# A state-space layer and a gated recurrence on one Trainium2 core: kernel setup and first states re-placed among the row statistics

## The chip, the cores and the metric

The kernel runs on one core of a Trainium2 chip as a single launch. The metric is the device time of the launch in microseconds. TensorE, VectorE, ScalarE, GpSimd and SyncE are called PE, DVE, ACT, POOL and SP, as in the profile. Each engine takes its own list of instructions strictly in order. An instruction that waits for a semaphore holds back everything behind it on its engine.

## The reference

Two sandwiched layers over x of shape (8, 2048, 512) in float32, cut to what matters:

```python
# first layer: layer norm, a diagonal-plus-low-rank state-space convolution, gelu
K  = _dplr_kernel(Bc, Cc, Pc, Qc, Lam, step_c, seq_len)        # (512, 2048)
Kf = jnp.fft.rfft(K, n=2 * seq_len, axis=-1)
uf = jnp.fft.rfft(r, n=2 * seq_len, axis=1)                    # r = _layernorm(x)
h1 = jnp.fft.irfft(uf * Kf.T[None], n=2 * seq_len, axis=1)[:, :seq_len]
x  = x + _layernorm(gelu(h1 + D[0] * r))
# second layer: layer norm, a gated recurrence over the first axis, a product, tanh
c  = sigmoid(xt @ wf.T + c @ uf.T + bf) * c + sigmoid(xt @ wi.T + c @ ui.T + bi) * tanh(xt @ wc.T + c @ uc.T + bc)
h  = tanh(x @ wo.T + c_final @ uo.T + bo)
x  = x + _layernorm(h)
```

## The kernel before

The convolution is done in 16 chunks of 128 steps. Inside a chunk it is a product with a triangular matrix T of samples of K. Across chunks it goes through a state of 128 numbers for each channel: `Gm` carries a chunk's input into the state, the power of the state matrix in `Ak` carries the state on, and the output matrix M reads it out. Channels are taken in 16 groups of 32. For group 0 there are 15 states (`state(0)` to `state(14)`) and 12 pieces of M (`outm(0, 0)` to `outm(0, 11)`), each made by PE, then rounded to a high f16 half by ACT (lines 1061 and 1072), then completed by a low half by DVE (lines 1428 and 1438). Every state but the first needs both halves of the state before it. `state(1)` and all after it also wait for `ak` 8, which is the eighth power of the state matrix split into halves by POOL (`power(7)`, lines 908 and 835).

**The stage in question** is the first 136 us, the row statistics. It reads x chunk by chunk (16 chunks, k from 0 to 15, three buffers `xt`) to get the mean and variance of each row. Of the eight rows per partition in a chunk DVE takes `NB` (`rows_of`: 4, 5 or 6; 5 for chunks 5 to 11, 6 from chunk 12) with one `bn_stats` each (line 1448) and one `bn_aggr` each (line 1460), and ACT takes the rest with a `total` pass (line 1039), a `mean` (lines 1043, 1044) and a `square_sum` pass (line 1049), closed by `var` (line 1097). POOL turns the variances of a chunk into inverse deviations (lines 934, 936) and then normalizes the inputs u of the first groups: `norm(n)` in quarters of a group (two instructions, lines 918 and 920) and, for the last four chunks of group 0, `norm_chunk(k)` (lines 927, 929). `norm(2)` makes the inputs of states 8 to 11. It stands in POOL's program behind the variance of chunk 11. SP loads chunk k when chunk k - 3 is done by both DVE and ACT (`load_x`, line 536).

**Between the chunks** DVE does the serial work that makes the matrices. `square(0)` to `square(6)` double a power of the state matrix (line 1348) and store it (line 1334); each needs a product by PE. `kernel_out`, `kernel_max` and `kernel_parts` (lines 1392 to 1422) take the samples of K, find powers of two for scaling, and write `Cst` and its halves `C16` (lines 1416 to 1418, the start of M), `Gm` (line 1420) and the scaled samples (line 1422, semaphore `kparts`), which SP stores to `kpad`, from where T is loaded.

**EARLY** says behind which chunk's statistics the first 14 states are made. In DVE a state follows rows 0, 2, 4 and the last of the chunk. In ACT the first state of a chunk stands ahead of the chunk's `total` pass (`early()` at line 1085) and the others stand ahead of one `square_sum` each. PE runs states and pieces in order with nothing between. After state 14 the loop over groups begins, PE's first product in it being line 1876, which needs the inputs of chunk 15 normalized.

```python
EARLY = {10: (0, 1, 2), 11: (3, 4), 12: (5, 6, 7), 13: (8, 9), 14: (10, 11), 15: (12, 13)}
w.wait_ge(s["ak"], 8)                      # PE, state_high, from state 1 on
if k in (7, 8):                            # POOL
    power(2 * k - 10)
    power(2 * k - 9)
if k in (3, 5, 7, 9, 11):
    norm(NORM_FIRST[(k - 3) // 2])         # 0, 4, 1, 5, 2
```

Of the kernel before, what the change touches and what calls it, by code (L numbers as in the profile page):

```python
# [12 lines left out]
MUL, ADD, SUB, MAX = ALU.mult, ALU.add, ALU.subtract, ALU.max  # L13
# [68 lines left out]

NORM_FIRST = [0, 4, 1, 5, 2, 6, 7]

EARLY = {10: (0, 1, 2), 11: (3, 4), 12: (5, 6, 7), 13: (8, 9), 14: (10, 11), 15: (12, 13)}


def rows_of(k):
# [167 lines left out]
def s4_lstm_program(nc, x, xr, xg, wts, cst, small, four, out):  # L256
    ctx = ExitStack()
    with ctx:
# [133 lines left out]
        Cst = take(512)  # L392
# [136 lines left out]
        def sync_program(e):  # L529
# [45 lines left out]
            for k in range(16):  # L575
                if k + 3 < 16:
                    load_x(k + 3)
                if k == 10:
                    w.wait_ge(s["kparts"], 1)
                    e.dma_start(kpad.ap().rearrange("(m p) s -> p m s", p=128), Kw.rearrange("p (m s) -> p m s", m=4)).then_inc(s["kp"], 16)  # L580
                if k in (1, 4, 6, 8, 9):
                    load_u((4, 1, 5, 2, 3)[(1, 4, 6, 8, 9).index(k)])
                if k == 12:
                    load_T(0, 0)
                    load_u(6)
                    load_u(7)
# [215 lines left out]
            for h in range(128):  # L802
                j, v, c, _ = head_at(h)
                b = unit(v)[0]
# [215 lines left out]
        def act_program(e):  # L1020
# [53 lines left out]
            for k in range(16):  # L1074
                NB = rows_of(k)
                steps = list(EARLY.get(k, ()))

                def early():
                    if steps:
                        j = steps.pop(0)  # L1080
                        state(j)
                        if j < len(PIECES_0):
                            outm(0, j)

                early()
                for b in range(NB, 8):
                    total(k, b, NB)
                mean(k, NB)
                if k == 7:
                    w.wait_ge(s["pk"], KERNEL["V"])  # L1090
                    e.activation(V, bank[0][:, 0:128], ACT.Copy).then_inc(s["ak_"], 1)
                    w.wait_ge(s["pk"], KERNEL["Gp"])
                    e.activation(Gs, bank[1][:, 0:128], ACT.Copy).then_inc(s["ak_"], 1)
                for b in range(NB, 8):
                    early()
                    square_sum(k, b, NB)
                c("var").activation(mvk[:, k, NB:8, 1], sums[:, k % 2, 2, 0:8 - NB], ACT.Copy, scale=1.0 / H).then_inc(s["var"], 1)
                if k == 1:
                    samples()
                if k == 4:  # L1100
                    w.wait_ge(s["pk"], KERNEL["inv0"])
                    e.activation(OE[:, 0].rearrange("p f s -> p (f s)"), bank[6][:, 0:256], ACT.Copy).then_inc(s["ak_"], 1)
                if k == 6:
                    w.wait_ge(s["pk"], KERNEL["inv1"])
                    e.activation(OE[:, 1].rearrange("p f s -> p (f s)"), bank[7][:, 0:256], ACT.Copy).then_inc(s["ak_"], 1)
# [197 lines left out]
        def dve_program(e):  # L1303
# [38 lines left out]
            def square(k):  # L1342
                now, nxt = EE[k % 2], EE[(k + 1) % 2]
                ps = bank[4 + k % 2][:, 0:256].rearrange("p (a n) -> p a n", a=2)
                w.wait_ge(s["sqo"], k + 1)
                if k >= 1:
                    w.wait_ge(s["sqo"], k)
                c("e0").scalar_tensor_tensor(nxt, now, 2.0, ps, MUL, ADD).then_inc(s["e0"], 1)
                if k == 6:
                    power(7, EE[1][:, 1, :])  # L1350
                else:
                    power(k + 1, nxt[:, 0, :])
# [45 lines left out]
            def kernel_max():  # L1398
                m3 = dg[0:3, 3:4]
                w.wait_ge(s["pk"], KERNEL["kdg"])  # L1400
                c().tensor_reduce(m3, bank[7][0:3, 0:128], AX.X, MAX).then_inc(s["dv"], 1)
                c().tensor_scalar(m3, m3, 1e-18, None, MAX).then_inc(s["dv"], 1)
                c().tensor_scalar(m3.bitcast(I32), m3.bitcast(I32), 0x7F800000, None, ALU.bitwise_and).then_inc(s["dv"], 1)
                c("kmx").tensor_scalar(dg[0:3, 4:7], ident[0:3, 0:3], m3, None, MUL).then_inc(s["kmx"], 1)

            def kernel_parts():
                v, rv, rk, y, m = (scale[:, i:i + 1] for i in (0, 3, 5, 6, 7))
                w.wait_ge(s["pk"], KERNEL["kdg2"])
                c().tensor_copy(scale[:, 0:3], bank[7][:, 128:131]).then_inc(s["dv"], 1)
                c().reciprocal(scale[:, 3:6], scale[:, 0:3]).then_inc(s["dv"], 1)  # L1410
                c().tensor_scalar(m, scale[:, 4:5], rv, 16.0, MUL, MUL).then_inc(s["dv"], 1)
                c().tensor_scalar(rk, rk, 4096.0, None, MUL).then_inc(s["dv"], 1)
                c().tensor_scalar(y, rk, m, None, ALU.min).then_inc(s["dv"], 1)
                c("gs").reciprocal(scale[:, 8:9], y).then_inc(s["gs"], 1)
                c().tensor_scalar(m, y, v, 32.0, MUL, MUL).then_inc(s["dv"], 1)
                c().tensor_scalar(Cst, Cst, m, None, MUL).then_inc(s["dv"], 1)
                c().tensor_copy(C16[:, 0, :], Cst).then_inc(s["dv"], 1)
                c("C16").tensor_tensor(C16[:, 1, :], Cst, C16[:, 0, :], SUB).then_inc(s["C16"], 1)
                w.wait_ge(s["ak_"], KERNEL["Gs"])
                c("Gm").tensor_scalar(Gm, Gs, rv, 2.0, MUL, MUL).then_inc(s["Gm"], 1)  # L1420
                w.wait_ge(s["kw"], 1)
                c("kparts").tensor_scalar(Kf[:, :, 127:255], Ks, y, None, MUL).then_inc(s["kparts"], 1)

            def state(n):
                g, k = divmod(n, 15)
# [14 lines left out]
            for k in range(16):  # L1440
                NB = rows_of(k)
                i = k % 2
                steps = list(EARLY.get(k, ()))
                for b in range(NB):
                    w.wait_ge(s[f"xt{k % 3}"], 16 * (k // 3 + 1))
                    if k >= 2:
                        w.wait_ge(s["aggr"], k - 1)
                    ins = e.bn_stats(st6[:, i, b, :], xt[k % 3][:, b, :])  # L1448
                    if b == NB - 1:
                        ins.then_inc(s["rows"], 1)  # L1450
                    if steps and (b % 2 == 0 or b == NB - 1):
                        j = steps.pop(0)
                        state(j)
                        if j < len(PIECES_0):
                            outm(0, j)
                    if b == 2 and k in (7, 8, 9):
                        square(2 * k - 12)
                w.wait_ge(s["rows"], k + 1)
                for b in range(NB):
                    ins = e.bn_aggr(mvk[:, k, b, :], st6[:, i, b, :])  # L1460
                    if b == NB - 1:
                        ins.then_inc(s["aggr"], 1)
                if k == 0:
                    sigma()
                if k == 1:
                    sigma2()
                if k == 2:
                    kappa2()
                if k == 3:
                    kappa_E(0)  # L1470
                    square_first()
                    kappa_E(1)
                    square(0)
                if k == 6:
                    square(1)
                if k == 7:
                    kernel_out()
                    square(3)
                if k == 8:
                    kernel_max()  # L1480
                    square(5)
                if k == 9:
                    kernel_parts()
            state(14)


# [261 lines left out]
        def pe_program(e):  # L1748
# [22 lines left out]
            def square(k):  # L1771
                now, bk = EE[k % 2], bank[4 + k % 2]
                w.wait_ge(s["e0"], k + 1)
                e.matmul(bk[:, 0:128], now[:, 1, :], now[:, 0, :], start=True, stop=True)
                e.matmul(bk[:, 128:256], now[:, 0, :], now[:, 1, :], start=True, stop=True).then_inc(s["sqo"], 1)
# [127 lines left out]
            w.wait_ge(s["ak_"], KERNEL["OE1"])  # L1903
            e.transpose(bank[7][0:3, 0:128], dg[:, 0:3], ident).then_inc(s["pk"], 1)
            square(5)
            square(6)
            w.wait_ge(s["kmx"], 1)
            e.matmul(bank[7][:, 128:131], one[0:3, :], dg[0:3, 4:7], start=True, stop=True).then_inc(s["pk"], 1)
            for k in sorted(EARLY):
                for j in EARLY[k]:  # L1910
                    state_in(j)
                    state_high(j)
                    state_low(j)
                    if j < len(PIECES_0):
                        outm(0, j)
# [210 lines left out]
```

## Time and profile before

| | |
|---|---|
| median of 3 runs | 2673.97 us (2672.85 to 2675.7) |
| profiled execution | 2672.62 us, of which the span of the trace is 2670.8 us |
| PE busy | 2564.2 us, 96% of the span |
| DVE, ACT, POOL busy | 71%, 57%, 39% |
| TensorE clock granted, mean | 0.98 of full |
| statistics stage | 0 to 136 us of the span |

The page divides the span into shares by engine; the chain of waits follows the work that ended last back to the start. The stage before 136 us is the one part where PE is not the busiest engine. Times in the text are microseconds from the start of the span.

### The profile page before, as it was taken

To read this page: it belongs to the slowest core of one execution; us is meant where nothing else is said; L and a number is where in the kernel's file an instruction comes from. 1 tells how busy PE (TensorE), PEld (TensorE's weight loads), DVE (VectorE), ACT (ScalarE), POOL (GpSimd) and SP (SyncE) were. 2 spreads that over 40 slices of the span, in tenths; PEclk is the share of its full clock that TensorE was granted. 3 is DMA by queue.
4 is the path that set the end of the run, shared out by engine and by line. 5 is a ranking of instruction groups with operands and counts; after the bars stand their busy time and mean duration, and the time that the engine had idled before them with its cause. 6 is when DMAs were issued, how large, how long until landed. Compare 5 with 4: busy or idle time off the path is not lost.

```text
span 2670.8 us, 55058 instructions
## 1 busy us (share of the span) xinstructions
PE 2564.2 (96%) x21507; PEld 2093.8 (78%) x21507; DVE 1894.5 (71%) x3406; ACT 1527.0 (57%) x2864; POOL 1054.2 (39%) x1496
## 2 busy tenths in 40 slices
PE   5499999997999999999999999999999999999998
PEld 4278888886888888888888888888888888544443
DVE  8855656558886777667778877767777673678778
ACT  8656767567665555555556755555555553345444
POOL 7768687625232232222333523222222220245445
PEclk9799999998999999999999999999999999999999
DMA  8779787889644554355547564345544451478777
GB/s 357 280 237 313 265 298 273 288 292 309 151 138 111 126 132 105 98 119 126 132 99 169 156 157 117 99 104 127 138 104 100 113 120 70 167 264 306 260 256 260
DMA packets 510213, 489.95 MB, mean 183 GB/s; under 512 B 275584, under 2 KB 406912, under 8 KB 502656
## 3 DMA queue, kind: packets, MB, share of 16 engines
q1 hardware_dynamic: 509952, 486.43, 60.9%
q8 instruction: 169, 2.77, 0.4%
q14 instruction: 92, 0.75, 0.1%
HBM read 270.60 MB, written 150.73 MB: 158 GB/s over the span
## 4 chain that ended last, share of the span: by engine, by line
PE 89%; POOL 3%; DVE 2%; ACT 2%; DMA 2%; issue 1%; SPq 0%; POOLq 0%; DVEq 0%; ACTq 0%
PE bank L1987 31%; PE bank L1997 29%; PE bank L2061 12%; PE bank L1876 4%; PE bank L1826 3%; PE bank L1884 3%; PE bank L1862 3%; PE bank L1838 2%; PE bank L2045 2%; PE bank L1846 1%; POOL big L832 1%; POOL big L936 1%; DMA big<-big 1%; DMA yd<-big 0%; DVE big L1448 0%
## 5 line engine op out<-in xcount | busy, mean ns | idle before, releaser
L1987 PE MATMUL bank<-big 128*128 128x256 f16 x8064 | 1080.2, 274 | 17.2 <-DMA big<-big 7.8
L1997 PE MATMUL bank<-big 128*128 128x256 f16 x7056 | 962.6, 273 | 0.0
L1987 PEld LDWEIGHTS bank<-big 128*128 128x128 f16 x8064 | 790.9, 98 | 114.5 <-ACT big L1268 9.2
L1997 PEld LDWEIGHTS bank<-big 128*128 128x128 f16 x7056 | 690.4, 98 | 79.9
L977 POOL TENSOR_SCALAR big<-big 128x1 f32<-128x1 f32 x253 | 107.6, 425 | 1092.8 <-DVE big L1561 812.1
L2061 PE MATMUL bank<-big 128*128 128x512 f16 x1536 | 332.2, 379 | 0.0
L1228 ACT ACTIVATE big<-big 128x512 f32<-128x512 f32 x384 | 289.6, 803 | 14.1 <-DVE big L1705 14.1
L2061 PEld LDWEIGHTS bank<-big 128*128 128x128 f16 x1536 | 150.3, 98 | 181.2
L1705 DVE TENSOR_TENSOR big<-bank,big 128x512 f32<-128x512 f32 x192 | 130.7, 681 | 195.2 <-PE bank L1997 193.2
L1160 ACT ACTIVATE big<-big 128x512 f32<-128x512 f32 x256 | 206.1, 808 | 104.2 <-POOL big L979 100.6
L1187 ACT ACTIVATE big<-big 128x512 f16<-128x512 f32 x248 | 150.7, 623 | 118.2 <-DVE big L512 73.3
L1697 DVE TENSOR_TENSOR big<-bank,big 128x512 f32<-128x512 f32 x192 | 131.4, 684 | 110.1 <-PE bank L1997 108.9
L1438 DVE SCALAR_TENSOR_TENSOR big<-bank,big 128x320 f16<-128x320 f32 (+6 forms) x237 | 109.1, 460 | 138.9 <-ACT big L1072 137.2
L978 POOL TENSOR_TENSOR big<-big 128x1 f32<-128x1 f32 x253 | 193.3, 764 | 21.1
L1251 ACT ACTIVATE big<-bank 128x256 f32<-128x256 f32 x192 | 72.4, 377 | 220.6 <-PE bank L1997 213.2
L1287 ACT ACTIVATE big<-big 128x512 f32<-128x512 f32 x128 | 80.6, 629 | 199.1 <-DVE big L1717 199.1
L1268 ACT ACTIVATE big<-bank 128x512 f32<-128x512 f32 x192 | 113.1, 589 | 132.1 <-PE bank L1997 96.5
L1585 DVE TENSOR_TENSOR big<-big 128x512 f16<-128x512 f32 x248 | 168.7, 705 | 11.9 <-ACT big L1187 11.0
L918 POOL TENSOR_TENSOR big<-big 128x1024 f32<-128x1024 f32 x63 | 150.8, 2394 | 39.5 <-DMA big<-xg 39.3
L1826 PE MATMUL bank<-big 128*128 128x256 f32 x480 | 149.0, 393 | 15.0 <-DVE big L1420 10.4
L1876 PE MATMUL bank<-big 128*128 128x128 f32 x1024 | 159.2, 278 | 2.1 <-POOL big L929 2.1
L1279 ACT ACTIVATE big<-bank 128x256 f32<-128x256 f32 x192 | 72.2, 376 | 149.6 <-PE bank L1997 143.7
(226 smaller groups left out, 3718.9 us busy)
## 6 DMA issues: line engine op xcount, KB each, us to landing
big<-xr SPq DMA_DIRECT2D x16, 2048.0 KB, 8.8
big<-xg SPq DMA_DIRECT2D x64, 512.0 KB, 7.8
big<-kpad SPq DMA_DIRECT2D x32, 1024.0 KB, 12.1
yd<-big SPq DMA_DIRECT2D x16, 2048.0 KB, 16.9
big<-x SPq DMA_DIRECT2D x128, 256.0 KB, 3.2
x1d<-big SPq DMA_DIRECT2D x128, 256.0 KB, 2.0
xtd<-big SPq DMA_DIRECT2D x64, 512.0 KB, 4.6
big<-xtd SPq DMA_DIRECT2D x64, 512.0 KB, 4.1
```

What stands on the lines that cost most here:

```text
L918: e.tensor_tensor(ug, ug, st(0), SUB).then_inc(s["sub"], 1)
L978: rp().tensor_tensor(st[:, 7:8], st[:, 7:8], mhalf, ALU.pow).then_inc(s["rp"], 1)
L1160: return e.activation(o, rows.rearrange("p (g h) -> p g h", g=NG) if len(rows.shape) == 2 else rows, ACT.Identity, bias=st[:, 6:7], scale= ...
L1187: e.activation(xs16[k][:, 0, :].rearrange("p (g h) -> p g h", g=NG), source(i), ACT.Copy).then_inc(s["xh"], 1)
L1228: e.activation(zt[g][:, r::2, :], zt[g][:, r::2, :], ACT.Tanh if g == 2 else ACT.Sigmoid, bias=bs[:, g, a + 2 * r:a + 2 * r + 1], scale=in ...
L1585: e.tensor_tensor(lo, source(i), hi, SUB).then_inc(s["xlo"], 1)
L1697: e.tensor_tensor(z[:, 0:2, :], bank_b(n - 1)[:, :].rearrange("p (q t) -> p q t", q=2), z[:, 0:2, :], ADD).then_inc(s["u1"], 1)
L1826: ins = e.matmul(o, Gm, u[g % 3][:, k].rearrange("p h b -> p (h b)"), start=True, stop=(k == 0))
L1876: e.matmul(o, T[t % 3][:, h % 16, :], u[g % 3][:, :, h, :], start=(q == 0), stop=False, skip_group_check=True)
L1987: ins = e.matmul(o, WX[2 * g + lw][:, q, kt, 128 * a:128 * a + 128], slot[u % 2][:, part, lx, k0 + kt, :], start=(first and kt == 0 and (l ...
L1997: ins = e.matmul(o, WC[2 * g + lw][:, q, kt, 128 * a:128 * a + 128], cc[unit(u)[1] % 2][:, qc, lx, kt, :], start=False, stop=end, skip_gro ...
L2061: ins = e.matmul(bank[n % NB_][:, :], xt4[r % NXR][:, lx, kt, 128 * c:128 * c + 128], Wo[:, lw, kt, :], start=(a == 0), stop=(a == 11))
```

## The change

Four things are done, with no change in what is computed:

1. DVE's chain that makes the matrices is placed inside chunks 7 and 8: `square(2)` after the first row of chunk 7, `square(3)` after its third, `square(4)`, `kernel_max`, `square(5)` and `kernel_parts` after rows 0, 1, 2 and 3 of chunk 8, and `square(6)` behind chunk 8's `bn_aggr`. Before, these stood in and behind chunks 7, 8 and 9.
2. In `kernel_parts`, `Gm` and the scaled samples are made ahead of `Cst` and `C16`.
3. `EARLY` begins with state 0 in chunk 9, and each chunk from 10 to 14 takes states that are one later. In chunk 9 DVE makes it behind the last row and ACT ahead of the first `square_sum`.
4. PE waits for `kmx` ahead of `square(6)`; SP stores the samples in its turn k = 9, not 10, and asks for T and two quarters of u in turn 11, not 12, which is ahead of or behind the loads of x by one place.

```diff
-EARLY = {10: (0, 1, 2), 11: (3, 4), 12: (5, 6, 7), 13: (8, 9), 14: (10, 11), 15: (12, 13)}
+EARLY = {9: (0,), 10: (1, 2, 3), 11: (4, 5), 12: (6, 7, 8), 13: (9, 10), 14: (11, 12), 15: (13,)}
...
-                if k == 10:
+                if k == 9:
                     w.wait_ge(s["kparts"], 1)
...
-                if k == 12:
+                if k == 11:
                     load_T(0, 0)
                     load_u(6)
                     load_u(7)
...
-                early()
+                if k > 9:
+                    early()
...
-                c().tensor_scalar(Cst, Cst, m, None, MUL).then_inc(s["dv"], 1)
-                c().tensor_copy(C16[:, 0, :], Cst).then_inc(s["dv"], 1)
-                c("C16").tensor_tensor(C16[:, 1, :], Cst, C16[:, 0, :], SUB).then_inc(s["C16"], 1)
                 w.wait_ge(s["ak_"], KERNEL["Gs"])
                 c("Gm").tensor_scalar(Gm, Gs, rv, 2.0, MUL, MUL).then_inc(s["Gm"], 1)
                 w.wait_ge(s["kw"], 1)
                 c("kparts").tensor_scalar(Kf[:, :, 127:255], Ks, y, None, MUL).then_inc(s["kparts"], 1)
+                c().tensor_scalar(Cst, Cst, m, None, MUL).then_inc(s["dv"], 1)
+                c().tensor_copy(C16[:, 0, :], Cst).then_inc(s["dv"], 1)
+                c("C16").tensor_tensor(C16[:, 1, :], Cst, C16[:, 0, :], SUB).then_inc(s["C16"], 1)
...
-                    if steps and (b % 2 == 0 or b == NB - 1):
+                    if steps and (b % 2 == 0 or b == NB - 1) and (k > 9 or b == NB - 1):
...
-                    if b == 2 and k in (7, 8, 9):
-                        square(2 * k - 12)
+                    if (k, b) == (7, 0):
+                        square(2)
+                    if (k, b) == (7, 2):
+                        square(3)
+                    if (k, b) == (8, 0):
+                        square(4)
+                    if (k, b) == (8, 1):
+                        kernel_max()
+                    if (k, b) == (8, 2):
+                        square(5)
+                    if (k, b) == (8, 3):
+                        kernel_parts()
...
                 if k == 7:
                     kernel_out()
-                    square(3)
                 if k == 8:
-                    kernel_max()
-                    square(5)
-                if k == 9:
-                    kernel_parts()
+                    square(6)
...
             square(5)
-            square(6)
             w.wait_ge(s["kmx"], 1)
             e.matmul(bank[7][:, 128:131], one[0:3, :], dg[0:3, 4:7], start=True, stop=True).then_inc(s["pk"], 1)
+            square(6)
```

## Rows read from the trace of the kernel before

**Rows 1.** The page's part 4, shares of the chain that ended last.
```profile
PE 89%; POOL 3%; DVE 2%; ACT 2%; DMA 2%; issue 1%; SPq 0%; POOLq 0%; DVEq 0%; ACTq 0%
```
**Rows 2.** Chain of waits, 129 to 137 us: start, us, engine, tile, line.
```profile
129.60 1.80 DVE big L1448 x3
131.42 0.52 DVE big L1460 x6
132.35 1.68 POOL big L936
135.77 1.20 PE bank L1876 x4
```
**Rows 3.** DVE by time: start, duration, line, operation, forms, [idle before <-releaser].
```profile
86.01 2.73 DVE L1418 TENSOR_TENSOR big<-big 128x512 f16<-128x512 f32 x1
89.21 1.82 DVE L1420 TENSOR_SCALAR big<-big 128x128 f32<-128x128 f32 x1 [0.47 <-DVE big L1418]
...
96.24 0.42 DVE L1428 SCALAR_TENSOR_TENSOR big<-bank,big 128x256 f16<-128x256 f32 x1 [1.67 <-ACT big L1061]
...
114.76 0.42 DVE L1428 SCALAR_TENSOR_TENSOR big<-bank,big 128x256 f16<-128x256 f32 x1
```
**Rows 4.** ACT by time, 92 to 107 us.
```profile
92.41 0.38 ACT L1061 ACTIVATE big<-bank 128x256 f16<-128x256 f32 x1 [14.20 <-PE bank L1826]
...
92.77 0.66 ACT L1039 ACTIVATE big<-big 128x512 f32<-128x512 f32 x1
...
95.82 0.38 ACT L1061 ACTIVATE big<-bank 128x256 f16<-128x256 f32 x1 [0.33 <-PE bank L1846]
...
97.62 0.38 ACT L1061 ACTIVATE big<-bank 128x256 f16<-128x256 f32 x1 [0.64 <-PE bank L1846]
...
105.90 0.21 ACT L1097 ACTIVATE big<-big 128x3 f32<-128x3 f32 x1
106.02 0.36 ACT L1061 ACTIVATE big<-bank 128x256 f16<-128x256 f32 x1
...
106.75 0.63 ACT L1039 ACTIVATE big<-big 128x512 f32<-128x512 f32 x1
```
**Rows 5.** POOL by time, 88 to 114 us.
```profile
88.27 2.69 POOL L920 TENSOR_TENSOR big<-big 128x1024 f32<-128x1024 f32 x1
...
91.25 1.90 POOL L936 TENSOR_TENSOR big<-big 128x8 f32<-128x8 f32 x1
...
94.41 0.43 POOL L835 TENSOR_TENSOR big<-big 128x128 f16<-128x128 f32 x1
...
95.14 1.67 POOL L936 TENSOR_TENSOR big<-big 128x8 f32<-128x8 f32 x1
...
110.86 2.37 POOL L920 TENSOR_TENSOR big<-big 128x1024 f32<-128x1024 f32 x1
```
**Rows 6.** PE by time, 94 to 115 us.
```profile
94.98 0.58 PE L1838 MATMUL bank<-big 128*128 128x256 f16 x2 [1.49 <-POOL big L835]
...
107.65 1.45 PE L1862 MATMUL bank<-big 128*128 128x512 f16 x3 [0.47 <-DVE big L1438]
...
113.28 0.70 PE L1826 MATMUL bank<-big 128*128 128x256 f32 x2 [1.72 <-POOL big L920]
...
114.14 0.81 PE L1862 MATMUL bank<-big 128*128 128x512 f16 x3
```
**Rows 7.** DVE's groups by form, 97 to 132 us: busy, mean ns | idle before.
```profile
L1428 DVE SCALAR_TENSOR_TENSOR big<-bank,big 128x256 f16<-128x256 f32 x12 | 5.0, 417 | 2.7 <-ACT big L1061 2.5
L1438 DVE SCALAR_TENSOR_TENSOR big<-bank,big 128x512 f16<-128x512 f32 x7 | 4.8, 689 | 1.2 <-ACT big L1072 1.0
```
**Rows 8.** The loads of x by SP (line 536), all 16.
```profile
DMA to landing us min/median/max: 7.5/8.8/21.7
```
**Rows 9.** Windows: length, busy us (instructions) by engine, granted clock, DMA share, GB/s.
```profile
110.00:120.00 10.00, 6.83 (x32) 3.60 (x30) 8.87 (x21) 7.54 (x23) 6.52 (x6) 0.94 0.87 346
...
128.00:136.00 8.00, 3.34 (x9) 1.87 (x10) 4.74 (x15) 2.86 (x8) 6.46 (x8) 0.51 0.12 23
```

## Prediction

> **What bounds the kernel now.** I read the page's chain of waits first. PE carries 89% of the chain that ended last [rows 1], and from 135.77 us on it is fed almost without a gap. The change touches nothing behind that point except through the time at which it comes. So the question is only when PE's first product of the group loop starts. The chain of waits just ahead of it is the second view: DVE's row statistics of chunk 15 end at 131.94 (131.42 + 0.52), POOL's inverse deviation follows and the normalization of chunk 15, and PE starts at 135.77 [rows 2]. From the end of DVE's last `bn_aggr` to PE's start is 3.83 us, and the change leaves that tail alone. SP's requests for the weights and for the next inputs wait for the same statistics, so they move with it. One microsecond at 131.94 is therefore one microsecond of the kernel.
>
> The third view is each engine in order of time from 60 to 136 us. Three readings matter there. ACT stands idle for 14.20 us until PE has the first state at 92.41 [rows 4]. PE then waits a second time, for POOL: the half of `power(7)` that starts at 94.41 and takes 0.43 lets `state(1)` go at 94.98 [rows 5, 6]. A third wait is PE's for `norm(2)`: that ends at 113.23 (110.86 + 2.37) and lets state 8 in at 113.28 [rows 5, 6]. These last two are POOL's, and they decide the case.
>
> **Part 1, the matrix chain on DVE.** It gives `Gm` earlier. In DVE's order the rows of chunk 7 and the squares come to: `square(2)` at 63.8 as before, `square(3)` near 67.6, `kernel_out` ended near 73.2, `square(4)`, `square(5)` at 73.8 and 77.9, `kernel_parts` from about 79.1. Its seven small instructions take 1.5, so `Gm` is there near 81, where line 1420 now ends at 91.03 (89.21 + 1.82) [rows 3]. The scaled samples wait for POOL to clear their buffer (about 82), and `C16` is there near 84.5. Two of these instructions are long now: 2.73 for line 1418, 1.82 for line 1420 [rows 3]. A like piece of work, line 1438 of the same width, takes 0.69 [rows 7], and each of the long ones runs until a 2.4 us instruction of POOL ends. In their new places POOL has no such instruction under way, so about 2.0 and 1.5 go. Against that `square(2)` waits about 1.2 for PE's product, the samples wait 0.9 for POOL, and one storing of a power will probably run into POOL's instruction at 85.66 (2.1). DVE then ends chunk 9 with state 0 near 92.3. The price or gain of all this on the path is nothing, because of Part 2: DVE comes to `state(1)` about 3 us before it can be made. That 3 us is the cover; if it were gone, each further microsecond of DVE's would count in full.
>
> The stretched instructions are where the Trainium skill bears on the case. The page "SBUF — State Buffer", section "Who interferes with whom", says that VectorE and GpSimd share a pair of ports, held for a whole instruction by whichever starts first while the other fully waits. The rows agree: 2.73 and 1.82 against 0.69. By that rule alone the change would look like a gain of some 3.5 us of DVE; it would be one only if DVE set the pace of this stretch, which is the first rival below.
>
> **Part 2, states one place earlier.** State 0 moves to chunk 9, and costs nothing there (ACT is idle). `state(1)` cannot move: it needs `power(7)` by POOL, whose list is full from 40 us on and in which nothing is moved. What POOL can gain is that two of its own instructions are not stretched: 2.69 against 2.37 and 1.90 against 1.67 [rows 5], 0.55 in all. I take 0.5; the ends are 0 and 0.7. So `state(1)` is rounded by ACT at 95.3 where it is 95.82 now [rows 4].
>
> What has changed is what stands behind it. Before, chunk 10 began on ACT with state 0, and the three `total` passes and the means (92.77 to 95.49, that is 2.72) [rows 4] ran while `power(7)` was awaited. Now chunk 10 begins with `state(1)`: ACT waits for POOL with these passes queued behind. The one wait of 14.20 becomes two, near 75 to 85 for state 0 and its piece of M, and near 88 to 95.3, with chunk 9's squares between them. Chunks 10 and 11 also hold one more state: 0.73 for its two instructions of ACT (106.02 to 106.75) [rows 4]. ACT was waiting 0.64 for PE in that stretch [rows 4], and that goes. Before, ACT closed chunk 11 at 106.1 (105.90 + 0.21), which is 10.3 after 95.82. Now it is 95.3 + 10.3 + 2.72 + 0.73 - 0.64 = 108.4: **+2.3**.
>
> **Part 3, what hangs on it.** POOL may only start the deviation of chunk 11, and behind it `norm(2)`, when ACT has closed chunk 11; then it needs 7.1 as before. `norm(2)` ends at 115.6, and state 8 enters PE there and not at 113.28 [rows 6]. But state 8 now belongs to chunk 12, whose last row and `bn_aggr` stand behind it on DVE. Before, DVE made state 8 at 114.76 [rows 3] with 17.18 us to go to 131.94. Now it makes it 2.3 later and has more to go: two more rows at 0.60 (1.80 for three) [rows 2], and one more aggregation, 0.43 to 0.52 [rows 2], less some 0.2 of a small wait. The sum at DVE's last aggregation is 2.3 + 1.2 + 0.5 - 0.2 = **+3.8**. DVE waits about 3.3 us for state 8, at a place where it now runs on.
>
> **The other parts.** SP: the store of the samples goes out near 92 and not at 100, ahead of u's third quarter; nobody waits for either before 116. Loads of x follow the chunks: chunks 13 and 14 are asked for about 2.5 later and have several microseconds of reserve. Chunk 15's can only be asked for when chunk 12 is done, near 119.5. With 7.5 to 8.8 to landing [rows 8] it lands by 128.3, and DVE wants it at 131. The T load and two u quarters now stand ahead of it, but they leave at 109. PE's `kmx` wait ahead of `square(6)` has 5 us of reserve. All at nothing; the bound for chunk 15's load is 1 us if it takes 13.
>
> **The sum.** The profiled execution took 2672.62: with 3.8 that is 2676.4. The median of the runs is 1.35 above the profiled one, so 2677.8 by the measure of the runs. The ends of the unknown terms are +2 (POOL gains 0.7 and handoffs are a bit quicker) and +5.3 (POOL gains nothing, a late load adds 1). Places where I chose: the 0.5 of POOL, and that ACT's idle in chunks 10 and 11 wholly vanishes.
>
> **Rivals.**
> - *DVE sets the pace* (faster). If the waits on ACT and for `norm(2)` are hidden, DVE is left with what it has to do. It reaches `state(1)` 0.5 earlier with two rows more to do (1.2) and loses the waits it now has behind 97 us, 2.7 + 1.2 [rows 7]. That gives 131.94 - 0.5 + 1.2 - 3.9, that is -3.2: 2670.8. For it: DVE runs with hardly a gap from 118 on. Against: POOL's list fixes `norm(2)` behind ACT's chunk 11. It decides if state 8 enters PE before about 112. To be faster by over 0.2% (5.3 us) needs more than DVE can give; only the clock at the restart of PE could add it.
> - *Half clock through the states* (slower). PE's granted clock was 0.94 from 110 to 120 and 0.51 from 128 to 136 [rows 9]; it fell to the lower level, 1.2 of 2.4 GHz, when PE had waited for statistics. The changed kernel makes PE wait from about 112 to 115.6 for `norm(2)`, so the fall may come there. A piece of M takes 1.45 at the lower level and 0.81 at the higher [rows 6]. State 8's own path then has some 1.5 more (its input 0.5, its products 0.4, its piece 0.6), and the three behind it perhaps 0.3 each: 3.8 + 2.4 = +6.2, 2680.2. It decides if the clock reads one half from 115 to 125.
> - *No effect*: both POOL gates stay where they are since ACT catches up, and the states merely sit in other chunks: 2674. For it: ACT was idle 14 us before. Against: that idle time lies ahead of the gate.
>
> **How the numbers follow.** Forecast, +2 to +5.3: 0.52. Half clock or a worse pile-up, over +5.3: 0.18. No effect, -1 to +2: 0.15. DVE pace, -5.3 to -1: 0.10. More than that: 0.05. A measurement of this kernel tells about 0.2% (5.3 us) from no change. So faster 0.05, within 0.2% 0.77, slower 0.18. For the range the half-clock case is taken in and the lower end reaches into the case of no effect and a part of DVE pace: 2671.5 to 2681.5.
>
> **What would show it.** Right: `Gm` near 81 us; ACT's first state near 82, but its second at 95.3, with ACT idle ahead of it and the `total` passes of chunk 10 behind it; the last `var` of chunk 11 near 108.4; state 8 entering PE near 115.7 released by POOL's line 920; DVE's wait of about 3 us there; the last `bn_aggr` near 135.7; the group loop starting near 139.6. Wrong: `state(1)` released by anything but POOL, DVE without a wait after 97, or a last `bn_aggr` before 132. A load of x shown as the releaser in chunk 15 would be a cost that I set at nothing.

## The result, and the profile after

The changed kernel takes 2678.01 us (median of 20 runs, 2676.09 to 2679.96) against 2674.36 for the kernel before (20 runs): a ratio of 1.0015, with a 95% interval of 1.0008 to 1.0022. It is slower by 3.65 us (about 2 to 6 by the interval). That is within the 0.2% that I had named as the edge of what can be told, and yet the interval, with 20 runs of each, leaves out no change. The profiled execution took 2677.86, its span 2676.0.

The page's chain, part 4, of the changed kernel (it answers to [rows 1]):

```profile
PE 88%; POOL 4%; DVE 2%; DMA 2%; ACT 2%; issue 1%; SPq 0%; POOLq 0%; DVEq 0%; ACTq 0%
```

These shares are rounded to whole points, a point being 27 us. A difference of 5 us can't be read from them. The chain of waits of the changed kernel, from the end of the last statistics (start, us, what; it answers to [rows 2]):

```profile
136.67 0.52 DVE big L1471 x6
137.27 0.26 POOL big L934
137.60 1.68 POOL big L936
139.34 0.74 POOL big L927
140.15 0.74 POOL big L929
140.88 0.14 issue
141.02 1.19 PE bank L1883 x4
```

DVE's last aggregation ends at 137.19, not 131.94, and PE begins the group loop at 141.02, not 135.77. The tail of 3.83 is the same in both. From there to the end of the span are 2535.0 us in both profiled executions (2676.0 - 141.02 and 2670.8 - 135.77). So the whole difference of the two profiles, 5.2, arises before the loop.

ACT by time in the changed kernel (start, us, [idle before <-releaser]; it answers to [rows 4]):

```profile
83.43 0.38 ACT L1061 ACTIVATE big<-bank 128x256 f16<-128x256 f32 x1 [7.12 <-PE bank L1833]
...
95.39 0.38 ACT L1061 ACTIVATE big<-bank 128x256 f16<-128x256 f32 x1 [7.84 <-PE bank L1853]
...
95.75 0.66 ACT L1039 ACTIVATE big<-big 128x512 f32<-128x512 f32 x1
...
108.23 0.20 ACT L1098 ACTIVATE big<-big 128x3 f32<-128x3 f32 x1
```

State 0 comes 9 earlier, at 83.43. State 1 comes at 95.39 where it came at 95.82, and only now do the `total` passes of chunk 10 begin. ACT closes chunk 11 at 108.43. The two gates stand on PE's list (they answer to [rows 6]), with state 8's piece of M at the end:

```profile
94.55 0.59 PE L1845 MATMUL bank<-big 128*128 128x256 f16 x2 [8.83 <-POOL big L835]
...
115.58 1.22 PE L1833 MATMUL bank<-big 128*128 128x256 f32 x2 [5.42 <-POOL big L920]
116.59 0.63 PE L1845 MATMUL bank<-big 128*128 128x256 f16 x2
117.02 0.42 PE L1853 MATMUL bank<-big 128*128 128x256 f16 x1
117.23 1.49 PE L1869 MATMUL bank<-big 128*128 128x512 f16 x3
```

PE now waits 8.83 for `power(7)` where it waited 1.49, since it has `Gm` early and nothing to do with it. It waits 5.42 for `norm(2)` where it waited 1.72. DVE by time (it answers to [rows 3]):

```profile
81.56 0.49 DVE L1418 TENSOR_SCALAR big<-big 128x128 f32<-128x128 f32 x1
...
83.67 0.69 DVE L1423 TENSOR_TENSOR big<-big 128x512 f16<-128x512 f32 x1
...
95.81 0.42 DVE L1429 SCALAR_TENSOR_TENSOR big<-bank,big 128x256 f16<-128x256 f32 x1 [5.37 <-ACT big L1061]
...
117.89 0.42 DVE L1429 SCALAR_TENSOR_TENSOR big<-bank,big 128x256 f16<-128x256 f32 x1 [4.18 <-ACT big L1061]
119.39 0.69 DVE L1439 SCALAR_TENSOR_TENSOR big<-bank,big 128x512 f16<-128x512 f32 x1 [1.07 <-ACT big L1072]
```

The two stretched instructions are short (0.49 and 0.69 against 1.82 and 2.73), and DVE spends what that saves, and more, in a wait of 5.37 for state 1. The granted clock (window's length, busy by engine, clock, DMA share, GB/s; it answers to [rows 9]):

```profile
110.00:120.00 10.00, 4.58 (x15) 2.70 (x15) 4.46 (x9) 4.06 (x12) 5.30 (x3) 0.66 1.01 353
120.00:128.00 8.00, 4.77 (x23) 2.19 (x21) 7.93 (x27) 7.64 (x24) 4.05 (x6) 1.00 0.81 314
```

### The profile page after: what moved, and what is told of

The parts are those of the page before. It is cut to its first block, busy times and chain, and to the rows that moved or that the text cites. A ratio compares the mean times of both kernels' runs of the same rounds, so it can differ in the third digit from the quotient of the medians.

```text
span 2676.0 us, 55058 instructions
## 1 busy us (share of the span) xinstructions
PE 2561.9 (96%) x21507; PEld 2091.7 (78%) x21507; DVE 1891.0 (71%) x3406; ACT 1527.4 (57%) x2864; POOL 1051.9 (39%) x1496
## 4 chain that ended last, share of the span: by engine, by line
PE 88%; POOL 4%; DVE 2%; DMA 2%; ACT 2%; issue 1%; SPq 0%; POOLq 0%; DVEq 0%; ACTq 0%
PE bank L1994 31%; PE bank L2004 29%; PE bank L2068 12%; PE bank L1883 4%; PE bank L1833 3%; PE bank L1869 3%; PE bank L1891 3%; PE bank L1845 2%; PE bank L2052 2%; PE bank L1853 1%; POOL big L936 1%; POOL big L832 1%; DMA big<-big 1%; DMA big<-wg 0%; DMA big<-wts 0%
```

## The experiments

My theory is that two things of POOL's decide: `power(7)` lets state 1 go, and `norm(2)`, behind ACT's chunk 11, lets state 8 go. What the change puts behind these two waits is lost. The rivals: the matrix chain on DVE itself costs, DVE is the pace anyway, or it is only TensorE's lower clock. Each run is one kernel; "loop" is the time at which PE's first product of the group loop starts in its profile, which is one execution. The median is over 6 to 20 executions, and the ratio is to the kernel before as measured beside that run (medians 2673.82 to 2674.36).

| run | loop, us | median, us | ratio to before, interval |
|---|---|---|---|
| before | 135.77 | 2674.36 | |
| changed | 141.02 | 2678.01 | 1.0015 (1.0008 to 1.0022) |
| 1 states put back | 135.99 | 2673.25 | 0.9997 (0.9988 to 1.0007) |
| 2 chunk 10's totals first | 140.03 | 2677.48 | 1.0013 (1.0003 to 1.0022) |
| 3 state 8 in chunk 13 | 139.96 | 2676.89 | 1.0011 (1.0001 to 1.0020) |
| 4 power first | 135.63 | 2673.41 | 0.9998 (0.9988 to 1.0007) |
| 5 before, power first | 134.59 | 2672.13 | 0.9992 (0.9983 to 1.0002) |
| 6 inputs by chunk | 135.98 | 2673.12 | 0.9996 (0.9986 to 1.0005) |
| 7 both gates | 132.59 | 2669.84 | 0.9983 (0.9973 to 0.9992) |
| 8 filled, 12 products | 141.80 | 2677.13 | 1.0014 (1.0005 to 1.0023) |
| 9 both gates, requests back | 130.52 | 2667.60 | 0.9975 (0.9965 to 0.9985) |
| 10 before, both gates | 129.33 | 2666.57 | 0.9971 (0.9959 to 0.9982) |
| 11 filled, 7 products | 139.77 | 2677.84 | 1.0015 (1.0006 to 1.0024) |
| 12 as 9, states put back | 129.94 | 2665.87 | 0.9970 (0.9958 to 0.9981) |

The loop's start moves over 12.5 us, and the median less the start stays between 2535.3 and 2538.6. So a microsecond of this stage is a microsecond of the kernel, but with about 1.6 either way that the stage does not explain. That spread lies behind the loop's start: in the profiled executions the part from there to the end took 2533.2 (run 12) to 2537.8 us (run 11). The stage itself repeats well. In the changed kernel and in runs 1, 2 and 3, which share the gate of state 1, ACT begins it between 95.39 and 95.56.

**Run 1, states put back.**

```diff
-EARLY = {9: (0,), 10: (1, 2, 3), 11: (4, 5), 12: (6, 7, 8), 13: (9, 10), 14: (11, 12), 15: (13,)}
+EARLY = {10: (0, 1, 2), 11: (3, 4), 12: (5, 6, 7), 13: (8, 9), 14: (10, 11), 15: (12, 13)}
```

> The changed kernel with only the distribution of the states over the chunks put back (state 0 in chunk 10, state 8 in chunk 13). Theory (what made it slower is the place of the states, not the matrix chain): the group loop starts at 135.4 us, 0.4 before the kernel before, since power(7) comes 0.4 earlier; total 0.4 below the kernel before, about 2674.0. Rival A (the earlier matrix chain on DVE, its collisions and the moved DMA requests cost the time): the loop still starts near 141, total near 2678.

The loop starts at 135.99, 5.0 earlier than in the changed kernel. The early matrix chain and the moved requests of SP cost next to nothing here; rival A is out. ACT still makes state 1 at 95.42, as in the changed kernel (ACT by time):

```profile
95.42 0.38 ACT L1061 ACTIVATE big<-bank 128x256 f16<-128x256 f32 x1 [7.86 <-PE bank L1853]
```

The 0.4 that I expected as a gain over the kernel before did not reach the loop. It was there at state 8's gate, 112.86 against 113.28, and was lost again right behind it (PE by time):

```profile
112.86 0.70 PE L1833 MATMUL bank<-big 128*128 128x256 f32 x2 [2.85 <-POOL big L920]
...
113.73 1.45 PE L1869 MATMUL bank<-big 128*128 128x512 f16 x3
```

The piece took 1.45 where it takes 0.81 in the kernel before [rows 6]: the clock had fallen to the lower level. Nearly all of the loss is the place of the states.

**Run 2, chunk 10's totals first.**

```diff
-                if k > 9:
+                if k > 10:
                     early()
```

> The changed kernel, but in chunk 10 ACT makes no state ahead of its total passes (state 1 follows them, ahead of the first square pass). Theory (ACT's passes of chunk 10, 2.7 us, queue behind the wait for power(7)): ACT closes chunk 11 near 105.8 and not at 108.4, norm(2) lets state 8 in at 112.9 and not at 115.6, the group loop starts at 138.3 and not at 141.0, total about 2675.3. Rival B (DVE is the pace from chunk 10 on): the loop starts within 0.5 of 141.0, total 2678.

The loop starts at 140.03: 1.0 is won, not 2.7. The passes do run ahead of the wait. But the three states of chunk 10 then follow each other with nothing in between to hide PE and DVE, and ACT waits 0.63, 0.62 and 0.20 between them (ACT by time):

```profile
95.47 0.38 ACT L1061 ACTIVATE big<-bank 128x256 f16<-128x256 f32 x1 [5.06 <-PE bank L1853]
...
97.27 0.38 ACT L1061 ACTIVATE big<-bank 128x256 f16<-128x256 f32 x1 [0.63 <-PE bank L1853]
...
99.09 0.38 ACT L1061 ACTIVATE big<-bank 128x256 f16<-128x256 f32 x1 [0.62 <-PE bank L1853]
```

ACT closes chunk 11 at 107.5 against 108.4. The passes in front of the wait are therefore one part of the 2.3. The rest, 107.5 against 106.1 in the kernel before, goes with one more state in chunks 10 and 11 (0.73) and with 0.8 more of waits between the states.

**Run 3, state 8 in chunk 13.**

```diff
-... 12: (6, 7, 8), 13: (9, 10), ...
+... 12: (6, 7), 13: (8, 9, 10), ...
```

> The changed kernel with state 8 alone put back into chunk 13 (which then has states 8, 9 and 10). Theory (DVE stands still for norm(2) with the last row and aggregation of chunk 12 queued behind): state 8 still enters PE at 115.6, but DVE has done one row, the aggregation and the first row of chunk 13 by then, 0.6 + 0.5 + 0.6 = 1.7: the group loop starts at 139.3, total about 2676.3. Rival C (only the half clock on state 8's path costs, 1.3): no gain, loop at 141.

The loop starts at 139.96, 1.1 earlier. DVE's wait for state 8 shrinks from 4.18 to 2.49, the 1.7 expected:

```profile
114.93 0.66 DVE L1449 BATCH_NORM_STATS2 big<-big 128x6 f32<-128x512 f32 x1
118.08 0.42 DVE L1429 SCALAR_TENSOR_TENSOR big<-bank,big 128x256 f16<-128x256 f32 x1 [2.49 <-ACT big L1061]
119.57 0.69 DVE L1439 SCALAR_TENSOR_TENSOR big<-bank,big 128x512 f16<-128x512 f32 x1 [1.07 <-ACT big L1072]
```

Some of it is given back: a wait of 0.22 at state 9, which now follows two rows later, and the gate itself 0.2 later. Rival C, that nothing is won, is out by the profile. The totals do not decide it: the ratios 1.0011 and 1.0015 have intervals that overlap.

**Run 4, power first.**

```diff
-                if k in (7, 8):
-                    power(2 * k - 10)
-                    power(2 * k - 9)
+                if k == 7:
+                    for j in range(4, 8):
+                        power(j)
```

> The changed kernel with POOL's power(6) and power(7) ahead of norm(1). Theory (state 1 is pinned by POOL's list): state 1 is made near 88.7 on ACT and not at 95.4; then the next thing late is POOL itself, norm(5) and then norm(2), so that state 8 enters PE near 110.6 and the group loop starts near 136.0; total 5 below the changed kernel, about 2673 to 2674. Rival B (DVE or the loads of x set the pace): state 1 comes early, but the loop starts at 139 or later and the total stays above 2676.

The loop starts at 135.63 and the total is 2673.41, 4.6 below the changed kernel. PE by time:

```profile
87.90 0.59 PE L1845 MATMUL bank<-big 128*128 128x256 f16 x2 [2.22 <-POOL big L835]
...
110.21 1.22 PE L1833 MATMUL bank<-big 128*128 128x256 f32 x2 [5.62 <-POOL big L920]
```

The gate of state 1 moves from 94.55 to 87.90, and the second gate follows it by 5.4, not by the full 6.7: by then POOL's own list is full. This is what I had named as the next thing late. How much of this is the change's loss, and how much a gain that the kernel before could have too, is told by run 5.

**Run 5, before, power first.** The same edit on the kernel before.

> The kernel before with POOL's power(6) and power(7) ahead of norm(1), nothing else changed. Theory (before, Gm and power(7) came nearly together, 91.0 and 94.8, and ACT ran its passes of chunk 10 meanwhile, so that the early power is of use only with an early Gm): state 1 is made on ACT at 95.5 and not at 95.8, the group loop starts between 135.0 and 135.8, total within 1 of the kernel before. Rival D (power first is worth 5 by itself, whatever DVE's order): loop near 131, total near 2669.

The loop starts at 134.59, 1.2 earlier; I expected 0 to 0.8. The interval of the total does not leave out no change. The place where the estimate fails is DVE's list:

```profile
85.75 0.80 DVE L1418 TENSOR_TENSOR big<-big 128x512 f16<-128x512 f32 x1
87.03 0.29 DVE L1420 TENSOR_SCALAR big<-big 128x128 f32<-128x128 f32 x1 [0.48 <-DVE big L1418]
```

With POOL's short instructions of `power` beside them, and `norm(1)` only from 88.15 on, both of the stretched instructions of [rows 3] are short, with DVE's order untouched. `Gm` is there at 87.3 and not at 91.0. So POOL's order is worth more than I had counted, for both reasons. Rival D's 5 is not there. State 8 does enter PE 2.6 earlier, at 110.66, but PE had waited 3.72 for it. The clock was at the lower level: from state 8's input to the end of its piece are 3.12 us (110.66 to 113.78), where the kernel before takes 1.67 [rows 6]. That takes back 1.4 of the 2.6.

Runs 4 and 5 are a pair with one order of POOL. The change costs 1.0 at the loop there (135.63 against 134.59) and not 5.2, though its state 8 enters PE 0.45 earlier. What is left, 1.5, is the two rows and the aggregation that stand behind state 8 in the changed kernel.

**Run 6, inputs by chunk.** Chunks 8 to 11 of group 0 are normalized like 12 to 15; the counts of `nrm` and `nrmc` follow.

```diff
-                if k in (3, 5, 7, 9, 11):
+                if k in (3, 5, 7):
                     norm(NORM_FIRST[(k - 3) // 2])
-                if k >= 12:
+                if k >= 8:
                     norm_chunk(k)
+                if k == 11:
+                    norm(5)
...
-                if g == 0 and k >= 12:
-                    w.wait_ge(s["nrmc"], k - 11)
+                if g == 0 and k >= 8:
+                    w.wait_ge(s["nrmc"], k - 7)
```

> The changed kernel, with group 0's inputs of chunks 8 to 11 normalized chunk by chunk as those of 12 to 15 are (state 8 then waits for chunk 8's statistics and not for those of chunk 11), norm(5) behind them. Theory (state 8's gate is worth DVE's waits of 4.2 and 1.1 there, the half clock included): state 8 enters PE without waiting for POOL, the group loop starts near 136, total near 2673. Rival B (DVE is behind anyway, or POOL's 1.4 more of work passes the wait on): loop at 139 or later.

The loop starts at 135.98, as expected. State 8 no longer waits for POOL, and the waits of 4.18 and 1.07 on DVE are gone, though state 1 is still held to 95.6. Either gate alone brings the changed kernel back to the loop start of the kernel before. For this gate there is no run of the kernel before with the same edit, so what it gains there is not known.

**Run 7, both gates.** Runs 4 and 6 together.

> The changed kernel with both of POOL's gates moved: power(6) and power(7) ahead of norm(1), and chunks 8 to 11 normalized chunk by chunk. Theory (the two gates are all that keeps the change from paying, then DVE is the pace): group loop near 130.5, total near 2668.5, that is 0.2% below the kernel before. Rival E (the loads of x, three buffers, become the next wait): a load of x is shown as the releaser of DVE or ACT in chunks 13 to 15 and the loop starts at 133 or later.

Loop at 132.59, total 2669.84. That is faster than before, but 2 are missing, and rival E names the cause: the load of x is the releaser, though the loop stays under the 133 that I had put to it. DVE by time in chunk 15 shows a load of x as the releaser:

```profile
124.23 0.69 DVE L1452 BATCH_NORM_STATS2 big<-big 128x6 f32<-128x512 f32 x1 [2.25 <-DMA big<-xr]
```

SP's requests by time (the second line is the load of chunk 15, which landed 10.4 later; the first of the two requests for u took 9.39 of the 9.87):

```profile
103.83 9.87 SPq L544 DMA_DIRECT2D big<-xg  x2
113.80 0.38 SPq L536 DMA_DIRECT2D big<-xr  x1
```

The load of chunk 15 could have been asked for at 110.2, when DVE had done chunk 12. SP was still in its request for u, which it had begun at 103.8 and which took nearly 10 us to leave. That is the change's own Part 4, moving T and two quarters of u ahead of this load.

**Run 8, filled with 12 products.**

```diff
                 for j in EARLY[k]:
+                    if j == 8:
+                        w.wait_ge(s["kmax"], 1)
+                        for _ in range(12):
+                            e.matmul(bank[6][:, 0:256], Gm, u[0][:, 0].rearrange("p h b -> p (h b)"), start=True, stop=True)
                     state_in(j)
```

> The changed kernel with 12 products whose result nobody reads put ahead of state 8 on PE, where it waits 5.4 for norm(2). Theory (1.3 of the loss is the lower clock on state 8's input, products and piece): the clock reads full from 111 on, state 8's piece takes 0.8 and not 1.5, the group loop starts near 139.7, total 1.3 below the changed kernel. Rival F (the clock there costs nothing): loop at 141.

The fill ran at the lower clock at first and took 7.2 us, to 117.9, past the gate. The lower level was there before the fill: the piece of M just ahead took 1.48, against 0.81 in the changed kernel. So the run does not answer its question by its time: the loop starts at 141.80, 0.8 later. Its rows do give the price: from state 8's input to the end of its piece are 1.57 us (117.93 to 119.50) against 3.14 in the changed kernel (115.58 to 118.72).

**Run 9, both gates, requests back.** Run 7 with SP's turn 11 put back to 12.

```diff
-                if k == 11:
+                if k == 12:
                     load_T(0, 0)
```

> The changed kernel with both of POOL's gates moved (power(6) and power(7) ahead of norm(1); chunks 8 to 11 normalized chunk by chunk) and SP's requests for T and for two quarters of u put back from turn 11 to turn 12, behind the load of x for chunk 15. Theory (in the run with both gates moved DVE waited 2.3 for the load of chunk 15, which SP asked for only at 113.8, when its request for u had gone out): the load goes out near 110.2, DVE does not wait for it, the group loop starts near 130.4, total near 2667.7, 0.23% below the kernel before. Rival G (DMA is the limit, not the order of requests): the loop stays at 132 to 133, total 2669.8.

The loop starts at 130.52, the total is 2667.60. The load goes out at 110.2 and DVE's wait for it is gone. The order of requests was the cause, and rival G is out.

**Run 10, before, both gates.** Runs 4 and 6 on the kernel before.

> The kernel before with the same two gates of POOL moved and nothing of the change. Theory (with the gates open DVE is the pace, and the early matrix chain with the states one place earlier is worth about what DVE's port collisions and waits in chunks 7 to 10 differ by, 1): loop start near 131.3, total near 2668.7. Rival H (the change is worth more or less than that by itself): a difference to the run with the change of over 2 either way.

Loop at 129.33, total 2666.57, where I expected 131.3. With the gates open the kernel without the change is 1.2 ahead of run 9 at the loop, and by the medians level with it. By this pair rival H, over 2 either way, is not there. But run 9 has a part of the change put back. Against run 7, which has the gates and the whole change, this run is 3.3 ahead both at the loop and by the medians, and so rival H does hold, on the side of the kernel without the change. The change has no gain of its own that needed only the gates opened.

**Run 11, filled with 7 products.** As run 8, with `range(7)`.

> The changed kernel with 7 products whose result nobody reads ahead of state 8 on PE (with 12 they ran to 117.9 and were themselves late). Theory (the lower clock costs 1.57 on state 8's path, 3.14 against 1.57 in the two runs): they end before norm(2), state 8 enters at 115.7 at the higher clock, the group loop starts near 139.5, total 1.5 below the changed kernel, 2676.5. Rival F (no gain): loop at 141, 2678.

This time the fill ends ahead of the gate and state 8 goes at the higher clock (an f32 product shows as two instructions, so the seven are x14):

```profile
110.18 3.19 PE L1921 MATMUL bank<-big 128*128 128x256 f32 x14
115.79 0.70 PE L1833 MATMUL bank<-big 128*128 128x256 f32 x2 [2.43 <-POOL big L920]
116.33 0.38 PE L1845 MATMUL bank<-big 128*128 128x256 f16 x2
116.55 0.27 PE L1853 MATMUL bank<-big 128*128 128x256 f16 x1
116.66 0.81 PE L1869 MATMUL bank<-big 128*128 128x512 f16 x3
```

The loop starts at 139.77, 1.25 earlier than in the changed kernel (1.5 less 0.2 for the gate, which came that much later). The median, 2677.84, does not show it: 1.25 is as large as what the stage leaves unexplained. In the profile the clock's price is shown; in the total it is not.

**Run 12, as run 9, states put back.**

> The changed kernel with the gates of POOL and SP's requests moved as in the run before last, and with the distribution of the states of the kernel before (state 0 in chunk 10, state 8 in chunk 13). Theory (with open gates it hardly matters where the states stand): loop start within 0.7 of 130.4, total 2667.5 to 2668.3. Rival I (states one place earlier pay once the gates are open): loop at 131.5 or later.

Loop at 129.94, total 2665.87, the lowest median of all, 0.9970 (0.9958 to 0.9981) of the kernel before. It is not told from runs 10 and 9 by its interval. It was expected at 130.4 within 0.7; the total came out 1.6 below the range I gave. Rival I is out: with the gates open the early place of the states costs 0.6 (run 9 against this one).

## Why the prediction was right or wrong

**The forecast of 2677.8 was met by 2678.01, but not by its sum alone.** I forecast +3.8 at the loop and in the total. The medians moved by 3.65, the profiles by 5.2. The profiled execution of before was the lower one of its kernel (2672.62 against 2674.36), and its median less its loop start is the highest of the table. The sum gave 2676.4 for a profiled execution, and 2677.86 was measured. The 1.35 that I added to come to the median was 0.15 in the changed kernel. The two errors cancel, so the agreement to 0.2 us is luck. That the time lies in the range is not: the interval of the loss, about 2 to 6 us, holds both the 3.8 and the 5.2.

**Part 1, the matrix chain on DVE, at nothing: right.** Run 1 has it with nothing else but SP's moves, and starts its loop within 0.2 of before. Sizes differed. `Gm` came at 82.05, not near 81. Most of that is one small instruction of `kernel_max` that was itself stretched beside POOL's, 1.14 where 0.30 stood before (DVE by time, changed kernel):

```profile
77.07 1.14 DVE L1405 TENSOR_SCALAR big<-big 3x3 f32<-3x3 f32 x1
```

The collision that I set at 2.1 for storing the last power did not happen: it began at 85.78, just ahead of POOL's 85.90, and took 0.31. DVE's cover was then 5.4 and not 3. By the Trainium skill ("SBUF — State Buffer", "Who interferes with whom") the instruction that starts first has the shared ports for its whole length, and the other waits. The trace agrees in these two: line 1405 ran to 78.21, and POOL's 2.36 us instruction, begun at 75.83, ended at 78.19; the store began ahead of POOL's long instruction and was not stretched. It does not hold for every pair: two of DVE's instructions just ahead of line 1405 took 0.14 each beside that same instruction of POOL. Removing the stretched instructions brought nothing here, because DVE did not set the pace.

**Part 2, +2.3 at the end of ACT's chunk 11: right in size.** State 1 came at 95.39 (forecast 95.3) and `var` ended at 108.43 (108.4). Runs 1, 2 and 4 show both halves of the mechanism: the gate, and what was queued behind it. Of the makeup of the 2.3 I had too simple a picture. Run 2 took the 2.72 of passes out from behind the gate and got 1.0, since the waits between states came back in their place.

**Part 3, norm(2) and state 8: right in mechanism, too small in size.** State 8 entered PE at 115.58 (115.6), DVE stood still there, 4.18 + 1.07 against the 3.3 expected. From that point to the last aggregation I had counted state 8's path at the speed of the kernel before. The term that failed is this one: it was 1.5 longer, as the clock had fallen to the lower level while PE waited 5.42 (granted 1.00 from 110 to 112 us, 0.63 from 112 to 115, 0.50 from 115 to 117). This was my half-clock rival, put at 0.18 with a price of 2.4. It came true for state 8 alone; the 0.3 that I gave each of the next three did not come, since the clock read 1.00 again from 120 on. The stage's sum is then 2.3 for the gate, 1.5 for the clock, and 1.4 for the added rows and aggregation net of waits (forecast 1.5): 5.2. Run 11 takes back 1.25 of the clock's part, and the pair of runs 4 and 5 shows the last term.

**Part 4, SP's requests, at nothing: right here, and with no cover once the rest is mended.** In the changed kernel the load of chunk 15 was asked for at 120.7 and DVE did not wait for it. In run 7 the same order cost 2.1.

**The rivals.** "DVE sets the pace" would have put the loop at 132.6; it was out by 8. "No effect" was out by the interval. Each gate alone (runs 4 and 6) brings the loop back to 135.6 and 136.0, so the loss of 5.2 needs both. But moving `power` is worth 1.2 to the kernel before as well (run 5), so not all that came back is the change's loss: in like surroundings the change costs 1.0 with `power` first, and 3.3 with both gates open (run 7 against run 10), of which 2.1 is the order of SP's requests.

What stays open is the 1.6 either way between the loop's start and the end, which none of these runs was made for, and what makes the clock fall where it does.

## What to carry to other kernels

Before a producer is made earlier, list everything its consumer waits for, and find the one that comes last. Here `Gm` came 9 us earlier and the second operand of the next step, one row of POOL's list further down, did not move. On an engine that takes its list in order, moving the consumer up as well is then worse than leaving it, because independent work ends up behind the wait. The remedy was on the other engine: with POOL's two powers taken up, 5.4 us came back. Then try the remedy without the change. The kernel before with both of POOL's gates moved took 2666.57 (run 10), less than the changed kernel with the same remedy (run 7, 2669.84).

## What the runs showed of the hardware that I had not expected

- A stretched instruction can be cured from either side. Line 1418 took 2.73 beside a 2.53 us instruction of POOL and 0.80 beside POOL's short ones (run 5). Even a 3 by 3 instruction was stretched from 0.30 to 1.14.
- A wait of 5.42 of PE's between two stretches of states cost the clock, and the path behind it took 3.14 instead of 1.57 to 1.68 (runs 8 and 11, 1.67 in the kernel before). In run 1 the level fell right behind a wait of 2.85; in the kernel before it did not fall at one of 1.72, and state 8 had its piece in 0.81 [rows 6]. A fill of 7 unread products with 2.43 of waiting behind it kept the higher level. The length of the last wait is not the whole of it: in the kernel before a piece ran at the lower level, 1.45, at 107.65 [rows 6] behind waits of only 1.33, 1.13 and 0.47. In run 8 the piece at 109.66 took 1.48 although its program up to there is that of the changed kernel.
- SP's two requests for u, 512 KB each, took 9.87 us to leave behind the request for T (run 7), and the next load of x, which could have left at 110.2, left at 113.8. The same two took 7.08 in the kernel before.
